# Two-layer attention and expert kernel: blocks without GpSimd's drain, fills by ScalarE, maxima 13 units ahead

## The reference, cut to what matters

```python
x = x + xattn0(layernorm(x), ctx)   # 8 heads of width 4
x = x + ffn0(layernorm(x))          # 8 experts, top 2, at most 640 rows each
x = x + xattn1(layernorm(x), ctx)   # 16 heads of width 16
x = x + ffn1(layernorm(x))          # 15 experts, top 3, and a shared expert
# xattn: q = xn@Wq+bq; k, v from ctx; softmax(q k^T * scale) v @ Wo + bo, over 512 keys
# ffn:   probs = softmax(xn @ Wr.T); top k; each expert's gated product on its tokens; weighted sum
```

## Time and profile before

| what | value |
|---|---|
| median of 3 runs | 1312.74 us (1309.6 to 1313.87) |
| the profiled execution | 1313.49 us, of which the span is 1311.8 us |
| PE busy | 1126.1 us, 86% of the span |
| DVE busy | 756.1 us, 58% |
| ACT busy | 517.8 us, 39% |
| POOL busy | 501.3 us, 38% |
| mean granted clock of PE | 0.908 of full speed |

### The profile page before, as it was taken

One profiled execution on the slowest core, in us unless ns is written; L12 is line 12 of the kernel. 1 busy time (PEld: TensorE's weight loads), 2 busy tenths in 40 slices (PEclk: granted clock), 3 DMA queues, 4 the chain that ended last, 5 costly groups with the idle time before them and its releaser, 6 DMA issues. The chain is left out here.

```text
span 1311.8 us, 20376 instructions
## 1 busy us (share of the span) xinstructions
PE 1126.1 (86%) x6704; PEld 751.3 (57%) x6705; DVE 756.1 (58%) x1435; ACT 517.8 (39%) x1068; POOL 501.3 (38%) x540
## 2 busy tenths in 40 slices
PE   4698897269999999999378898989867999999997
PEld 1233344159999999999353344444444555555554
DVE  5876713735765576564477877768329344444427
ACT  2175553133543354343024665647524222222220
POOL 6403236445664565340203334220204146565510
PEclk9598877669999999999687898989878999999999
DMA  4122204433322332110453342322073332222233
GB/s 157 33 90 90 74 17 146 139 99 110 121 87 77 103 119 89 62 50 6 150 141 99 81 130 49 104 69 67 18 272 120 137 118 72 75 77 77 65 141 116
DMA packets 68640, 126.21 MB, mean 96 GB/s; under 512 B 16113, under 2 KB 34328, under 8 KB 67798
## 3 DMA queue, kind: packets, MB, share of 16 engines
q1 hardware_dynamic: 58486, 100.86, 23.7%
q0 software_dynamic: 10080, 24.38, 5.7%
HBM read 90.23 MB, written 38.01 MB: 98 GB/s over the span
## 5 line engine op out<-in xcount | busy, mean ns | idle before, releaser
L672 ACT ACTIVATE PT<-S 128x512 f32<-128x512 f32 x384 | 207.8, 599 | 156.9 <-PE S L650 155.0
L687 DVE TENSOR_REDUCE M<-S 128x2 f32<-128x1024 f32 x192 | 229.8, 1222 | 52.3 <-PE S L626 51.7
L660 PE MATMUL PV<-PT,VA 128*32 128x256 f32 x1536 | 131.3, 431 | 6.8 <-ACT OSB L679 5.6
L532 DVE TENSOR_TENSOR HTl<-HF,HTh 128x320 fp32r<-128x320 f32 x128 | 128.7, 1005 | 1.0
L2077 PE MATMUL bank<-W,XST 128*128 x248 | 121.0, 610 | 6.1 <-issue 3.7
L626 PE MATMUL S<-KS,QS 62*128 62x512 f32 x384 | 101.7, 498 | 23.5 <-DVE M L687 19.7
L650 PE MATMUL S<-QS,KS 64*128 64x512 f32 x384 | 116.8, 538 | 3.6 <-ACT PT L672 3.6
L501 ACT ACTIVATE SG<-Gm 128x320 f32<-128x320 f32 x128 | 56.0, 437 | 116.8 <-PE Um L459 115.6
L538 DVE TENSOR_TENSOR HF<-Um,SG 128x320 f32<-128x320 f32 x128 | 62.4, 487 | 65.1 <-ACT SG L501 65.1
L359 POOL TENSOR_TENSOR w12l<-stage,w12h 128x1024 fp32r<-128x1024 f32 x32 | 77.1, 2410 | 57.0 <-ACT w12h L353 56.7
L472 PE MATMUL Ym<-w3h,HTh 128*128 128x256 f32 x320 | 93.4, 292 | 0.0
(11 more groups left out here) (267 smaller groups left out, 2381.4 us busy)
## 6 DMA issues: line engine op xcount, KB each, us to landing
stage<-in_W12T SPq DMA_DIRECT2D x32, 512.0 KB
stage<-in_W3T SPq DMA_DIRECT2D x16, 512.0 KB
W<-in_fc1T SPq DMA_DIRECT2D x2, 3840.0 KB, 17.9
scrk<-kparts SPq DMA_DIRECT2D x24, 256.0 KB
KS<-scrk SPq DMA_DIRECT2D x32, 192.0 KB, 4.2
scrq<-parts SPq DMA_DIRECT2D x24, 256.0 KB
QS<-scrq SPq DMA_DIRECT2D x32, 192.0 KB, 3.4
YG<-yk SPq DMA_DIRECT2D x4, 1536.0 KB, 14.0
```

The source lines that it names most:

```text
L532: dve.tensor_tensor(HT[1][:, j, at], HF[:, c % HFS, :], HT[0][:, j, at].bitcast(F32), ALU.subtract).then_inc(h_done, 1)
L660: m = pe.matmul(self.PV[VW * h:VW * (h + 1), at], self.VA[:, g, kt, VW * h:VW * (h + 1)], self.PT[:, kt, h, at], start=(kt == 0 and s == 0 ...
L672: act.activation(self.PT[:, kt, 2 * j + h, :], self.S2[:, n % 3, :], ACT.Exp, scale=self.lay.scale).then_inc(self.exp_done, 1)
L687: dve.tensor_reduce(self.M[:, g % 2, :, h, q], got, AX.X, ALU.max).then_inc(self.ring.dve_free, 1)
```

## The change

1. The blocks of `layer0`, `experts0`, `layer1` and `recycle` are opened with `no_gpsimd_drain=True`; `ffn1`'s is not. The semaphore of the scatters of `experts0` is made outside its block.
2. In `layer0` ScalarE fills KS and VA instead of GpSimd; in `layer1` ScalarE fills them instead of DVE. Both copy a tile of ones, broadcast.
3. In `layer0` DVE normalises element 1 as well as 0, and the order at the start is kv 0, xn 0, vt 0, q 0, xn 1, q 1, kv 1, vt 1. SP loads K rows as soon as they are stored, and Q rows after them.
4. Step S computes the unit S + 13 of maxima (16 before), so 13 units come before the first scores. `turn` and `negate` of the next group move from step 1 to step 4.
5. `TURN_XF`, `ROUTE` go from 18, 21 to 21, 24; `TURN_XF0`, `ROUTE0` from 15, 17 to 18, 20.
6. In `layer1` GpSimd's adds for element b+2 stand in the groups j = 0 and 2 (1 and 2 before), and the bias and the norm for the router stand ahead of them in the loop.

```diff
+AHEAD = UNITS + 5
+def ahead(S, NG):
+    n = S + AHEAD
+    return divmod(n, UNITS) if n < UNITS * NG else None
-        block = ctx.enter_context(nc.Block())
+        block = ctx.enter_context(nc.Block(no_gpsimd_drain=True))
-TURN_OT, PROJECT, TURN_XF, ROUTE = 6, (9, 11), 18, 21
+TURN_OT, PROJECT, TURN_XF, ROUTE = 6, (9, 11), 21, 24
-TURN_OT0, PROJECT0, TURN_XF0, ROUTE0 = 6, (8, 9), 15, 17
+TURN_OT0, PROJECT0, TURN_XF0, ROUTE0 = 6, (8, 9), 18, 20
...
             store("k", 0)
+            sp.wait_ge(stacks_done, 2)
+            sp.wait_ge(stored[0], 48)
+            for g in range(2):
+                at.load(sp, g, "k")
             store("q", 0)
-            load(0)
-            load(1)
+            sp.wait_ge(stored[0], 96)
+            for g in range(2):
+                at.load(sp, g, "q")
+            store("q", 1)
             store("k", 1)
-            store("q", 1)
...
-            pool.memset(at.KS[:, :, :, :].bitcast(F32), 1.0).then_inc(stacks_done, 1)
-            pool.memset(at.VA[:, :, :, :], 1.0).then_inc(va_ones, 1)
-            for b in range(1, BATCH):
+            for b in range(2, BATCH):
                 norm_root_pool(pool, link, pre, b)
...
-            for u in range(1, UNITS):
+            for u in range(1, AHEAD - UNITS):
                 at.maxima(pe, 1, u)
...
-                        if g + 2 < NG:
-                            at.maxima(pe, g + 2, i)
+                        if ahead(S, NG):
+                            at.maxima(pe, *ahead(S, NG))
...
-                        if i == 1 and g + 1 < NG:
+                        if i == 4 and g + 1 < NG:
                             at.turn(pe, g + 1)
...
+            act.copy(at.KS[:, :, :, :].rearrange("p s h (a c) -> p (s h a) c", c=P),
+                     env.ones[:, :].unsqueeze(1).to_broadcast([P, SLOTS * 2 * TPB, P])).then_inc(stacks_done, 1)
+            act.copy(at.VA[:, :, :, :].rearrange("p g t c -> p (g t) c"),
+                     env.ones[:, :].unsqueeze(1).to_broadcast([P, NG * TPB, P])).then_inc(va_ones, 1)
...
             norm_apply(dve, pre, X, XN[:, 0:TPB, :], 0)
+            first_stats(1)
             dve.wait_ge(kv_loaded, 64)
             low_keys(0)
-            first_stats(1)
+            norm_root(dve, link, pre, 1)
+            norm_apply(dve, pre, X, XN[:, TPB:2 * TPB, :], 1)
...
                 if b + 2 < BATCH:
-                    if j in (1, 2):
-                        adds(b + 2, j - 1)
+                    if j in (0, 2):
+                        adds(b + 2, j // 2)
```

More of the change, by code:

```diff
@@ L726, in ring1 @@
     names = [("xn", 0), ("q", 0, 0), ("q", 0, 1)] + [("max", 0, u) for u in range(UNITS)] + [("max", 1, 0), ("turn", 0)]
-    names += [("max", 1, u) for u in range(1, UNITS)]
+    names += [("max", 1, u) for u in range(1, AHEAD - UNITS)]
     for g in range(NG):
@@ L1327, in _ @@
             at.negate(dve, 0)
-            for u in range(1, UNITS):
+            for u in range(1, AHEAD - UNITS):
                 at.reduce(dve, 1, u)
-            at.halve(dve, 1)
             for g in range(NG):
@@ L1336, in _ @@
                         S, o = UNITS * g + i, UNITS * j + i
[L1337 to L1341, removed]
+                        if ahead(S, NG):
+                            n, u = ahead(S, NG)
+                            at.reduce(dve, n, u)
+                            if u == UNITS - 1:
+                                at.halve(dve, n)
+                        if i == 4 and g + 1 < NG:
                             at.negate(dve, g + 1)
@@ L1590, in _ @@
                         add_bias(b + 2)
[L1591 to L1595, removed]
             pool.wait_ge(bo_added, NT)
@@ L1848, in _ @@
                         o = 8 * j + 2 * kt + s
[L1849 to L1853, removed]
+                        if ahead(UNITS * g + 2 * kt + s, NG):
+                            n, u = ahead(UNITS * g + 2 * kt + s, NG)
+                            at.reduce(dve, n, u)
+                            if u == UNITS - 1:
+                                at.halve(dve, n)
+                        if (kt, s) == (2, 0) and g + 1 < NG:
                             at.negate(dve, g + 1)
@@ L2342, in recycle @@
     used = sorted(s if isinstance(s, int) else s.num for s in nc.released_uncleared_semaphores)
-    with nc.Block() as block:
+    with nc.Block(no_gpsimd_drain=True) as block:
         @block.gpsimd
@@ L2377, in program @@
         env.expert = sb("expert", [1, TILES1], I32)
+        env.xs0_loaded, env.y0_stored = [sem(f"xs_loaded{i}m0") for i in range(2)], sem("y_storedm0")
         env.mult = sb("mult", [P, E1, FF1 // P])
@@ L2398, in program @@
             env.place = places(ROOM0, "0")
-            env.XS0, env.xs0_loaded = env.place("XS", [P, 2, CAP0 // P, D]), [sem(f"xs_loaded{i}m0") for i in range(2)]
+            env.XS0 = env.place("XS", [P, 2, CAP0 // P, D])
             env.rows_stored = [sem(f"rows_stored{b}0") for b in range(2)]
```

58 lines of the change are left out of this document (33 added, 25 removed).

## The result

The changed kernel takes 1267.0 us, median of 4 runs (1263.2 to 1272.3), beside 1313.3 us (1309.6 to 1315.0) for the kernel before. The ratio is 0.965, with a 95% interval of 0.961 to 0.970. The profiled execution took 1268.39 us, its span is 1266.7 us, 45.1 us less than before. Its mean granted clock is 0.928 (before 0.908).

What follows compares the result with a forecast made beforehand. PE was taken to set the pace, with DVE near; block ends 7.8, start 6.0, units 4.8 and XF 13.0, less 0.5 for the turn, gave 31.1 us less: 1282 us forecast, range 1271 to 1298.

Steps and rivals of the forecast that it cites:

- The steps (XF, turn, the units' give-back): Both layers' steps: XF's later turn gains 13.0 us, the turn in step 4 costs 0.5, three late units cost 2.0.
- rival (c): Steps: without XF waits PE's granted clock rises and DVE's backlog goes, another 8 us, 1274 us; chance 0.13.
- XF alone: PE's waits for GpSimd's XF in both layers: three steps later removes most, 13.0 us gained, bounds 7 and 16.
- Block ends: Ends of layer0 and experts0: without the drain 2.8 and 5.0 us go, 7.8 together, bounds 0 and 8.8.
- the meeting and the jump alone: Layer1 to ffn1: DVE's 0.80 us gap, GpSimd long idle, taken as a block end's cost without the drain.
- Start: Start of layer0: L121 freed of GpSimd's fills, element 1 on DVE, first reduce at 31.6; gain 6.0 us, bounds 2 and 8.
- Units and turn: Three fewer units save 6.8 us before first scores, 2.0 back later; turn in step 4 costs 0.5 net.
- NM's landing: Next group's scores: NM lands 2.1 us after issue, at 897.3, a second to spare; no group waits.
- Rival (a): Steps: DVE is the pace, so units give nothing net and half of XF's gain returns; 1296 us; chance 0.18.
- (b): Block ends: the gaps are code fetch, not drain, so 7.8 us stay; 1290 us; chance 0.10.
- (d): Step 0 of 22 groups: NM's transfer becomes the pace; at 4.8 us landing it costs 37, 1319 us; chance 0.05.
- (e): Start of layer0: L121's 5.72 us has another cause, 5 us stay, 1287; inside the forecast's 0.54 chance.

Runs made afterwards that it cites:

- b_fill: Kernel before with ten dummy 128x128 products on PE in front of each of the five XF waits, nothing moved: 1300.4 us, ratio 0.9910.
- b_blocks: Kernel before with only the four block ends freed of the drain and the scatters' semaphore made outside its block: 1304.4 us, ratio 0.9933.
- b_start: Kernel before with only the start changed (fills on ACT, element 1 on DVE, new order of first items): 1304.5 us, ratio 0.9921.
- b_xf_units: Kernel before with XF's turn and router later, thirteen units ahead and the maxima's turn in step 4, nothing else: 1285.0 us, ratio 0.9784.
- b_xf: Kernel before with only XF's turn and the router three steps later: 1287.1 us, ratio 0.9808.
- a_warm: Changed kernel with one dummy product of 512 columns and 62 rows behind each unit of the prologues: ratio 0.9661 to the kernel before.
- a_warm128: Changed kernel with dummy products of the 128x128 identity in the prologues, eight ahead and one behind each unit: ratio 0.9717 to the kernel before.

## Why the prediction was wrong in size

By spans 45.1 us were gained and 31.1 forecast. By the forecast's own steps:

- **The steps (XF, turn, the units' give-back), where it failed.** Forecast: -13.0 + 0.5 + 2.0 = 10.5 us less. Measured: 16.7 less. In its parts the forecast was 12.5 us less standing and 2.0 more busy; measured are 8.6 less standing and 8.0 less busy. So the step that failed is that the sum took PE's products to cost the same after the change: they cost 10.0 us less than it had, at a higher granted clock. That the standing was put 3.9 us too high hid a part of this. XF's waits went as priced, but the waits for DVE's reduce rose by 4.8 us, where 1.5 taken off XF's gain and 0.5 for the turn had left 2.0 for it. b_fill shows that the clock answers to what PE does in a wait, since filling the waits, without ending them, gives 12 us. The prediction had the clock as rival (c), with 8 us and a chance of 0.13.
- **XF alone.** Forecast 13.0 with bounds 7 and 16, measured 25 us alone and 19 (spans) to 21 (medians) inside the change. All its waits went; three steps were enough.
- **Block ends.** Forecast 7.8, measured 4.8 + 5.6 = 10.4. The drain was the cause. Too small was "the last gather": I subtracted a meeting of 0.80 us from the gap, as if PE had to start behind the issue of the last gather. Without the drain GpSimd's queued gathers no longer hold the meeting, and PE starts while they are still being issued (b_blocks). Nor is 0.80 us "the meeting and the jump alone": at the end of layer1 DVE's gap is 0.39 or 0.40 in all ten traces without the drain and 0.78 to 0.89 in six of the seven with it (0.32 in b_fill).
- **Start.** Forecast 6.0, measured 8.3; 7.2 alone (b_start). L121 and the second element went as reckoned. I took query 0 and 1 at the length of the earlier trace rows, 3.19 us, the low clock, and in the profiled execution both ran in 1.90. Part of the 8.3 is the luck of that execution: by the ten traces with the new start it can be 6.6 to 8.6.
- **Units and turn.** The prologues gave 7.4 us (4.0 and 3.4; 6.8 forecast). The new wait before the output turn is there in full, 11.8 us for 11.4. The turn alone changes nothing net, as forecast, but only because the clock gives 6.5 us for 3.5 of standing. On top of XF the clock has little more to give: the steps of b_xf_units are 6.9 us longer than those of b_xf (381.0 and 374.1), 6.7 of it standing, which is about what its prologues save.
- **NM's landing.** It never held the scores, but the 2.1 us of the earlier trace rows that the prediction calls a small DMA's is of a store of 256 KB. NM's own DMAs have 8 KB, and no trace shows when they land, so the second to spare stays a guess that came out.
- **Not additive.** Alone the four parts give 9 + 10 + 11 + 25 = 55 us, together 46. Most of the difference is between XF and the units with the turn (36 alone, 28 together): it is the clock's share, which each brings alone and the two together bring mostly once.

The misses add up: steps 6.2, block ends 2.6, start 2.3, prologues 0.6, and 2.3 us elsewhere, nearly all in layer0's end besides the block (granted clock there 0.72, before 0.68), together 14.0. Rival (a), DVE as the pace, would have shown as waits for the reduce above 20 us in layer1; at L649 and L635 they are 11.3, and 14.1 in all. Rival (c) had the right mechanism in its first half, the clock, and too small a size; its second half, that DVE's backlog goes, isn't seen. Rivals (b), (d) and (e) fell with b_blocks, with the absence of a wait for NM, and with the 0.17 us of L121.

## What to carry to other kernels

Where the rows show the granted clock below 1 in the stretch behind a wait of TensorE, a change of its waits can be worth more than their length (here 15 us of waits gave 25 alone), and two changes that both raise the clock get most of it only once. A dummy product inside the wait, with nothing moved, is a cheap way to find out how much of it is clock, but the dummies tried in the changed kernel, in the prologues and in waits under 1 us, gained nothing. At a block end, ask what the next block's first work really waits for, and whether GpSimd's queued issues must be behind the meeting at all.

## What was not expected of the hardware

- Ten dummy products in each of five waits made the kernel before 12 us faster (ratio 0.9910), and eight turns behind them took 1.05 us and not 1.97.
- PE was busy 13.39 of 14.50 us with products of 62 rows at a granted clock of 0.50 (a_warm). With dummies of 128 rows between them it fell from 1.00 to 0.50 during the prologue and stayed there for 12 us with PE busy 11.50 (a_warm128).
- Without the drain GpSimd's gathers go on across a block end: the last began 0.23 us after PE's first product of the next block.
- An elementwise operation of DVE on 128x4 took 5.72 us beside GpSimd's fills and 0.17 without the last two of them. The Trainium skill (SBUF — State Buffer, Who interferes with whom) gives a lock between the two engines for this; the runs agree, though none here varies the operation's mode alone. L121 began at 6.71 during the fill of KS, which ended at 8.95, and came free only when the fill of VA behind it ended, at 12.40: the lock, if it is one, held over two of GpSimd's instructions.
